# Two-layer gated cross-attention and expert kernel: loads of 100, 116, 119 and 121 rows are issued as a piece of a multiple of sixteen rows and a rest

## The chip, the cores and the metric

One core of a Trainium2 chip runs the whole program. The metric is the device time of one execution in microseconds (us). The core has five instruction streams: TensorE (PE, with its weight loads listed apart as PEld), VectorE (DVE), ScalarE (ACT), GpSimd (POOL) and SyncE (SP). SP computes nothing here: it issues nearly all the transfers, in order, and the transfers run on the core's 16 DMA engines. POOL issues a few transfers too, above all the scatters by row index.

## The reference

The input `x` is 8 batches of 100 tokens of 256 numbers, all float32, with a context of 8 x 361 rows of 256. Four blocks follow one another; `g_xattn` and `g_ffn` give a gate for each, applied through tanh.

```python
def _L0_xattn_ref(query, key, value, mask, Wq, bq, Wk, bk, Wv, bv):
    Q = jnp.einsum('nkm,dm->nkd', query, Wq) + bq
    Kp = jnp.einsum('nkm,dm->nkd', key, Wk) + bk
    V = jnp.einsum('nkm,dm->nkd', value, Wv) + bv
    scores = jnp.einsum('nqd,nkd->nqk', Q, Kp) / jnp.sqrt(jnp.float32(DQ))
    scores = jnp.where(mask, jnp.float32(-1000000000.0), scores)
    w = jax.nn.softmax(scores, axis=2)
    y = jnp.einsum('nqk,nkd->nqd', w, V)
    return y
...
    shared = jax.nn.silu(x @ w_gate.T) * (x @ w_up.T) @ w_down.T
    out = shared + expert_out.sum(axis=0)
```

1. Layer 0 cross-attention over the context with one head, with a mask.
2. Layer 0 feed-forward: a shared gated unit and 16 experts, of which each token takes the one with the highest router logit.
3. Layer 1 cross-attention over the context with 16 heads of 16.
4. Layer 1 feed-forward, itself a block: rotary self-attention with 16 heads, then a normalisation, a shared gated unit of 512 and 8 experts in 2 groups of 4. A token belongs to one group, takes two experts of it, and the sum goes through an RMS normalisation and is added to the token.

## The kernel before, in words

The kernel is one block with a stream for each engine. Order is written out by hand: every dependence is a semaphore, and a transfer adds 16 to its semaphore when it has landed. A token tile has 100 rows (`T = 100`), one for each batch, eight in all, and rows are tokens: `x` and `hN` are 100 rows of 8 x 256. The context is cut into pieces of 121, 121 and 119 rows (`KEYS = 121`). The experts of the last block work on tokens sorted by group, in eight tiles of 116 rows (`ET = 116`, `NX = 8`).

**The start** (SP L403 to L424). SP issues `x`, then the constants, three weights of 256 KB, the two biases, the gates and the bias row `row_bv`, then the mask and the context in three groups of batches, each group two transposed loads and three loads of rows (L412, L415). TensorE's first instruction waits for the weights and the constants together:

```python
pe.wait_ge(s("ld_w0"), 64)
pe.wait_ge(s("ld_const"), 64)
```

The last load that these two count is `row_bv`. DVE's first instruction (L1068) waits for `x` alone, POOL (L616) for the mask, and TensorE's scores for each group of the context.

**Between the layers** (SP L494 to L499, DVE L1206 to L1217). The first layer's experts scatter their rows to `yt_dram`. When the last scatter has landed, SP loads them back as tokens into `hN`, in two halves of four batches. DVE adds a half to `x` (`second_residual`, L1211), takes the statistics (L1050), POOL takes the root (L606) and DVE normalises (L1063). TensorE transposes the rows (L1509) and makes the queries, which go out to `qx_dram` and come back in another layout before the second attention starts.

**Before the sorted experts** (SP L561 to L564). POOL scatters the tokens, each row with 256 numbers, its token number and ten logits, to `es_dram` in sorted order (L734). When all have landed, SP loads them back in four pairs of tiles of 116 rows into `sorted_rows`, a part of `ctxbuf`. Each pair has a semaphore `b_xg`. Meanwhile TensorE makes the second product of the shared unit, 64 recorded products with `wdn`. Then, pair by pair, TensorE transposes (L1990) and ACT copies the result out (L1018); pair g must wait until ACT has emptied the bank of pair g - 2. DVE, after adding the shared result to the tokens (L1421, eight times), waits for all four pairs:

```python
for g in range(NX // 2):
    dve.wait_ge(s(f"b_xg{g}"), 32)
```

and begins the routing: the token numbers (L1424), the maxima and differences of the logits (L1425 to L1431, then `e_gx`), the exponentials on ACT behind its four copies (L1021, which loads an activation table first), and a chain of some 25 small DVE operations up to the weights of the experts (L1464). Only then does DVE multiply the hidden units (L1468). TensorE has made the hidden units of the first three of eight units of work by then and can go no further: the fourth needs a bank that the first L1468 empties.

**The end** (SP L569 to L588). `load_base` (L570) and `load_rest` (L574) bring the shared results and the tokens in sorted order, four loads each of 116 rows, used by DVE at L1475 and L1493. POOL scatters the result (L754).

Of the kernel before, what the change touches and what calls it, by code (L numbers as in the profile page):

```python
# [19 lines left out]
KT = D // 128  # L20
KEYS = 121
NJ = 3
# [36 lines left out]
Y_BANKS = [4, 5, 2, 3, 6, 7, 0, 1]  # L59
HIDDEN = [3 * 4, 3 * 4 + 2, 3 * 4 + 3] + [4 * 4] * 5  # L60


# [100 lines left out]
def build(nc, A, out):  # L163
# [4 lines left out]
    with ctx:  # L168
# [233 lines left out]
        def _(sp):  # L402
            sp.dma_start(x[:], A["x"]).then_inc(s("ld_x"), 16)  # L403
            sp.dma_start(consts[:], A["consts"]).then_inc(s("ld_const"), 16)
# [4 lines left out]
            def load_context(g):  # L409
                a, z = GROUPS[g]  # L410
                for k in range(KT):
                    sp.dma_start(ctxT[:, k, a:z, 0:CTX], A["ctxT"][128 * k:128 * k + 128, a:z]).then_inc(s(f"ld_ctx{g}"), 16)  # L412
                for j in range(NJ):
                    n = min(KEYS, CTX - KEYS * j)
                    sp.dma_start(ctxN[0:n, a:z, j, :], A["ctx"][a:z, KEYS * j:KEYS * j + n, :].rearrange("b p d -> p b d")) \  # L415
                        .then_inc(s(f"ld_ctx{g}"), 16)

            for i, n in enumerate(("g_xattn", "g_ffn")):
                sp.dma_start(gates[:, 2 * i:2 * i + 2], A[n].partition_broadcast(128)).then_inc(s("ld_const"), 16)
            sp.dma_start(brow["bv"][:], A["L0_xattn_bv"].partition_broadcast(128)).then_inc(s("ld_const"), 16)  # L420
            sp.dma_start(mask8[:], A["mask"]).then_inc(s("ld_mask"), 16)
            sp.wait_ge(s("filled"), FILL["pads"])
# [73 lines left out]
            for half in range(2):  # L496
                sp.dma_start(hN[:, NB // 2 * half:NB // 2 * (half + 1), :],
                             yt_dram[HALF * half:HALF * (half + 1), :].rearrange("(b t) d -> t b d", t=T)) \
                    .then_inc(s(f"b_yt{half}"), 16)  # L499
            def load_k(b, part):  # L500
# [61 lines left out]
            for g in range(NX // 2):  # L562
                sp.dma_start(sorted_rows[0:ET, 2 * g:2 * g + 2, :],
                             es_dram[2 * ET * g:2 * ET * (g + 1), :].rearrange("(i p) d -> p i d", p=ET)).then_inc(s(f"b_xg{g}"), 16)  # L564
            sp.wait_ge(s("e_bst"), 16 * (NB + 1))
# [3 lines left out]
            def load_base(g):  # L569
                sp.dma_start(hF[0:ET, 2 * g:2 * g + 2], eb_dram[2 * ET * g:2 * ET * (g + 1), :].rearrange("(i p) d -> p i d", p=ET)) \  # L570
                    .then_inc(s(f"ld_F{g}"), 16)

            def load_rest(g):
                sp.dma_start(xF[0:ET, 2 * g:2 * g + 2], ex_dram[2 * ET * g:2 * ET * (g + 1), :].rearrange("(i p) d -> p i d", p=ET)) \  # L574
                    .then_inc(s("ld_x"), 16)

# [14 lines left out]
        def _(pool):  # L591
# [19 lines left out]

            pool.wait_ge(s("ld_mask"), 16)
            for b in range(NB):
# [423 lines left out]
        def _(dve):  # L1037
# [27 lines left out]

            dve.wait_ge(s("ld_x"), 16)
            for b in range(NB):
# [140 lines left out]
            def second_residual(half):  # L1208
                dve.wait_ge(s(f"b_yt{half}"), 16)
                for b in range(NB // 2 * half, NB // 2 * (half + 1)):  # L1210
                    nc.vector.scalar_tensor_tensor(out=x[:, b, :], in0=hN[:, b, :], scalar=tg[0:T, 2:3], in1=x[:, b, :],  # L1211
                                                   op0=ALU.mult, op1=ALU.add).then_inc(s("b_res"), 1)
# [209 lines left out]
            for g in range(NX // 2):  # L1422
                dve.wait_ge(s(f"b_xg{g}"), 32)
            nc.vector.tensor_copy(tok[0:ET, :], sorted_rows[0:ET, :, D]).then_inc(s("b_tok"), 1)  # L1424
# [45 lines left out]
            for i in range(NX):  # L1470
                dve.wait_ge(s(f"ld_F{i // 2}"), 16)
                for p in range(2):
                    v = 2 * i + p
                    dve.wait_ge(s("e_down"), NB + v + 1)
                    link(nc.vector.scalar_tensor_tensor(out=hF[0:ET, i, :], in0=PB[Y_BANKS[v % 8]][0:ET, 0:D], scalar=we[:, i, 2 * p:2 * p + 1],  # L1475
                                                        in1=hF[0:ET, i, :], op0=ALU.mult, op1=ALU.add))
                    if v == 2 * NX - 1:
                        dve.wait_ge(s("e_down"), NB + v + 2)
                    nc.vector.scalar_tensor_tensor(out=hF[0:ET, i, :], in0=PB[Y_BANKS[(v + (v == 2 * NX - 1)) % 8]][0:ET, D:2 * D], scalar=we[:, i, 2 * p + 1:2 * p + 2],
                                                   in1=hF[0:ET, i, :], op0=ALU.mult, op1=ALU.add).then_inc(s("e_comb"), 1)  # L1480
                    dve.wait_ge(s("e_comb"), v + 1)
                for part, (a, z) in enumerate(FPARTS):
                    if i != z - 1:
                        continue
                    dve.wait_ge(s("f_sq"), z)
                    nc.vector.tensor_scalar(stdF[:, a:z], rsumF[:, a:z], 1.0 / D, RMS_EPS, ALU.mult, ALU.add) \
                        .then_inc(s("n_var"), 1)
                    dve.wait_ge(s("n_std"), roots("f", part))
                    dve.wait_ge(s("ld_x"), 16 * (1 + NX // 2))
                    for k in range(a, z):  # L1490
                        link(nc.vector.scalar_tensor_tensor(out=hF[0:ET, k, :], in0=hF[0:ET, k, :], scalar=rstdF[:, k:k + 1],
                                                            in1=growF[0:ET], op0=ALU.mult, op1=ALU.mult))
                        nc.vector.tensor_tensor(xF[0:ET, k, :], xF[0:ET, k, :], hF[0:ET, k, :], ALU.add).then_inc(s("f_out"), 1)  # L1493
# [3 lines left out]
        def _(pe):  # L1497
# [52 lines left out]
            for i in range(NB + 4):  # L1550
# [9 lines left out]
                if i < NB:  # L1560
                    b = i
                    if b >= 3:
                        pe.wait_ge(s("a_max"), b - 2)
                    for g, (a, z) in enumerate(GROUPS):
                        if a == b:
                            pe.wait_ge(s(f"ld_ctx{g}"), 16 * (KT + NJ))
                    for n in range(KT):
                        last = mm(PB[SB[b % 3]][0:T, 0:CTX], tT[:, n, T * b:T * b + T], ctxT[:, n, b, 0:CTX],
                                  n == 0, n == KT - 1)
                    last.then_inc(s("a_s"), 1)  # L1570
# [126 lines left out]
            pe.wait_ge(s("ld_wc"), 16 * 7)  # L1697
            pe.wait_ge(s("ld_ctx0"), 16 * (KT + NJ + KT))

# [125 lines left out]
            for half in range(3):  # L1825
                for _ in BEFORE[half][n if half == 0 else 0:]:
                    if EARLY[n] == KS[BACK[1][0]][0]:
                        pe.wait_ge(s("ld_ctx1"), 16 * (KT + NJ + KT))
                    early(n)
                    n += 1  # L1830
# [150 lines left out]
            for g in range(NX // 2):  # L1981
                pe.wait_ge(s(f"b_xg{g}"), 32)
                if g < 2:
# [90 lines left out]
```

## Time and profile before

| what | us |
|---|---|
| median of 3 runs | 556.81 (556.79 to 558.48) |
| the profiled execution, its own time | 556.68 |
| its span | 554.9 |
| PE busy in the span | 503.3 (91%) |
| DVE busy | 277.3 (50%) |
| ACT busy | 188.4 (34%) |
| POOL busy | 160.9 (29%) |

The execution's own time is 1.78 us above its span: what lies around the span is not in the trace. Times in the trace count from the span's start. The profiled execution lies 0.13 us below the median of the runs, so what is predicted from its trace stands for the median too. The largest of the three runs lies 1.67 us above the other two.

### The profile page before, as it was taken

What the parts mean: (1) busy time and instruction counts of PE and PEld (TensorE: products, weight loads), DVE (VectorE), ACT (ScalarE), POOL (GpSimd) and SP (SyncE); (2) the same over time, 40 slices, a digit from 0 to 9 for tenths busy, and PEclk for the clock granted to TensorE, in tenths of its full rate; (3) what the DMA queues carried; (4) which work ended last, traced back from release to release, by engine and by line L of the source; (5) the groups of instructions that cost most, each with busy time, mean ns of one, the idle gap of its engine ahead of it and who ended that gap; (6) DMA issues with size and microseconds to landing.
All of it is one profiled execution on the core that took longest, in us unless ns stands there. A gap on an engine that the chain in (4) does not pass through costs nothing.

```text
span 554.9 us, 9313 instructions
## 1 busy us (share of the span) xinstructions
PE 503.3 (91%) x3392; PEld 334.6 (60%) x3392; DVE 277.3 (50%) x664; ACT 188.4 (34%) x443; POOL 160.9 (29%) x179
## 2 busy tenths in 40 slices
PE   1989889899999889999999989899999988999992
PEld 1636565445556558887877767778867564444441
DVE  2436553112222767565576877988743214323452
ACT  1233331121112436555555554646652103110000
POOL 3122005001016306422241562543200666000232
PEclk9799978999999999999999999999999997999997
DMA  8978992269976987887555209300000233002100
GB/s 220 220 200 282 389 335 57 80 215 395 386 258 210 257 187 211 217 203 186 144 138 138 55 2 332 124 2 2 2 1 0 68 129 121 18 17 68 27 11 24
DMA packets 51790, 82.33 MB, mean 148 GB/s; under 512 B 10340, under 2 KB 40428, under 8 KB 51643
## 3 DMA queue, kind: packets, MB, share of 16 engines
q1 hardware_dynamic: 45967, 69.58, 42.2%
q0 software_dynamic: 5776, 12.13, 6.9%
q8 instruction: 29, 0.48, 0.4%
q14 instruction: 18, 0.15, 0.1%
HBM read 66.87 MB, written 15.15 MB: 148 GB/s over the span
## 4 chain that ended last, share of the span: by engine, by line
PE 73%; DVE 12%; issue 4%; DMA 4%; ACT 2%; SPq 1%; POOL 1%; POOLq 0%; DVEq 0%; ACTq 0%
PE pb L1499 68%; DVE hN L1063 2%; DVE nmx L1360 1%; DMA row_bv<-in_L_xattn_bv 1%; DMA qx_dram<-big_r 1%; DVE prob L1363 1%; PE pb L1910 1%; DMA hN<-yt_dram 1%; DVE bn L1050 1%; POOL rstd L606 1%; PE pb L1770 1%; DVE ctxbuf L1290 1%; PE pb L1680 1%; DVE nmx L1268 1%; DVE x L1211 1%
## 5 line engine op out<-in xcount | busy, mean ns | idle before, releaser
L1499 PE MATMUL pb<-split 128*100 128x362 f32 (+2 forms) x320 | 77.5, 326 | 4.0 <-DVE nmx L1268 2.7
L1499 PE MATMUL pb<-ring,big 128*116 (+1 forms) x232 | 76.8, 578 | 1.1 <-ACT big L822 1.1
L1268 DVE TENSOR_REDUCE nmx<-pb 100x1 f32<-100x361 f32 x128 | 62.8, 527 | 21.4 <-PE pb L1499 20.9
L1499 PEld LDWEIGHTS pb<-split 128*100 128x100 f32 (+2 forms) x320 | 55.5, 181 | 13.7 <-DVE nmx L1268 5.3
L1499 PEld LDWEIGHTS pb<-ring,big 128*116 128x116 f32 (+1 forms) x232 | 31.2, 162 | 43.2 <-issue 40.6
L939 ACT ACTIVATE big<-pb 121x400 f32<-121x400 f32 (+1 forms) x96 | 48.3, 505 | 20.5 <-PE pb L1499 17.9
L691 POOL TENSOR_TENSOR shift<-consts,nmx 100x400 fp32r<-100x400 f32 x32 | 28.2, 882 | 75.0 <-DVE nmx L1268 74.9
L1499 PE MATMUL pb<-big,arena 121*32 121x100 f32 (+3 forms) x1072 | 47.4, 261 | 1.7 <-ACT arena L789 1.2
L1499 PEld LDWEIGHTS pb<-big,arena 121*32 121x32 f32 (+3 forms) x1072 | 28.7, 112 | 18.2 <-issue 6.9
L1499 PE MATMUL pb<-hT,wgu 128*128 128x400 f32 (+1 forms) x100 | 35.8, 505 | 0.3 <-DVE hN L1346 0.3
L1499 PE MATMUL pb<-shift 100*121 100x400 f32 (+1 forms) x96 | 35.0, 364 | 0.0
L606 POOL TENSOR_TENSOR rstd<-std,minus_half 100x2 f32<-100x2 f32 (+3 forms) x11 | 11.0, 1000 | 71.9 <-DVE std L1058 46.0
L1499 PE MATMUL pb<-wdn,big 128*100 128x256 f32 x128 | 29.2, 380 | 1.4 <-issue 1.4
L1499 PE MATMUL pb<-ctxbuf 128*100 128x100 f32 x256 | 28.0, 253 | 0.0
L1499 PE MATMUL pb<-big,ring 128*128 128x464 f32 x64 | 27.8, 596 | 0.2 <-DVE big L1468 0.2
L1499 PEld LDWEIGHTS pb<-ctxbuf 128*100 128x100 f32 x256 | 26.1, 168 | 1.4 <-issue 0.8
L1499 PEld LDWEIGHTS pb<-hT,wgu 128*128 128x128 f32 x100 | 19.5, 206 | 12.1 <-issue 3.1
L660 POOL TENSOR_TENSOR ctxbuf<-tT,consts 128x1600 f32<-128x1600 f32 x8 | 24.4, 3045 | 7.4 <-PE pb L1499 7.4
L1499 PEld LDWEIGHTS pb<-wdn,big 128*100 128x100 f32 x128 | 20.8, 167 | 7.4 <-issue 2.0
L638 POOL DMA_INDIRECT yt_dram<-arena,tok x8 | 7.8, 978 | 59.3 <-ACT arena L841 59.3
L1499 PE MATMUL pb<-arena 128*100 128x256 f32 (+1 forms) x40 | 11.9, 433 | 13.6 <-DMA row_bv<-in_L_xattn_bv 12.0
L982 ACT ACTIVATE prob<-prob 100x400 f32<-100x400 f32 x32 | 17.2, 539 | 19.5 <-DVE prob L1363 19.2
(274 smaller groups left out, 844.1 us busy)
## 6 DMA issues: line engine op xcount, KB each, us to landing
ring<-in_L_ffn_gate_up_proj SPq DMA_DIRECT2D x12, 1024.0 KB, 10.1
split<-kx_dram SPq DMA_DIRECT2D x64, 181.0 KB, 3.9
ring<-in_L_ffn_down_proj SPq DMA_DIRECT2D x12, 512.0 KB, 7.9
kx_dram<-split POOLq DMA_DIRECT2D x16, 362.0 KB, 4.0
ctxbuf<-in_L_ffn_gate_up_proj SPq DMA_DIRECT2D x4, 1024.0 KB, 10.3
ring<-in_L_ffn_W_experts SPq DMA_DIRECT2D x4, 1024.0 KB, 13.3
split<-qx_dram SPq DMA_DIRECT2D x64, 50.0 KB, 2.1
ctxbuf<-in_ctxT SPq DMA_DIRECT2D x6, 361.0 KB
```

The lines of the kernel that those rows point to most:

```text
L606: nc.gpsimd.tensor_tensor(to[:, a:z], var[:, a:z], minus_half[0:var.shape[0], a:z], ALU.pow) \
L638: nc.gpsimd.indirect_dma_start(yt_dram, bass.IndirectOffsetOnAxis(tok[:, i:i + 1], 0), yb[:, i % 2, :], None, bounds_check=NT - 1, oob_is_ ...
L660: nc.gpsimd.tensor_tensor(qbd[:, b % 2].rearrange("p k (h t) -> p k h t", h=8), q, m, ALU.mult) \
L691: nc.gpsimd.tensor_tensor(diag[:, t % 2].rearrange("t (h q) -> t h q", h=4), ident[0:T, 0:T].unsqueeze(1).to_broadcast([T, 4, T]), nmx[:, ...
L939: nc.scalar.activation(pTq[0:KEYS_OF[j], t % 2, j, :], PB[ST[j]][0:KEYS_OF[j], 0:4 * T], ACT.Exp) \
L982: nc.scalar.activation(prob4[:, n % 3, :], prob4[:, n % 3, :], ACT.Exp).then_inc(s("d_p"), 1)
L1050: nc.vector.bn_stats(bn6[:, b, :], x[:, b, :]).then_inc(s("stats"), 1)
L1063: nc.vector.tensor_scalar(hN[:, b, :], x[:, b, :], mv[:, b, 0:1], rstd[:, b:b + 1], ALU.subtract, ALU.mult).then_inc(s("n_hN"), 1)
L1211: nc.vector.scalar_tensor_tensor(out=x[:, b, :], in0=hN[:, b, :], scalar=tg[0:T, 2:3], in1=x[:, b, :], op0=ALU.mult, op1=ALU.add).then_inc ...
L1268: nc.vector.tensor_reduce(nmx[:, t % 4, q:q + 1], PB[SB[n % 3]][0:T, 0:CTX], AX.X, ALU.max, negate=True) \
L1290: link(nc.vector.tensor_tensor(w4, w4, sin, ALU.mult))
L1499: return nc.tensor.matmul(o, l, r, start=start, stop=stop)
```

## The change

Every load whose number of rows sixteen does not divide is issued as two: one of the largest multiple of sixteen rows, one of the rest. A helper gives the two ranges of rows. The waits count two transfers where they counted one. Nothing else is changed: no bytes are added, no load changes its place in the order, and the rest follows right behind its piece in SP's stream. Names and lines in the text are those of the kernel before.

```diff
+def by16(rows):
+    return [(0, rows // 16 * 16), (rows // 16 * 16, rows)]
...
-            sp.dma_start(x[:], A["x"]).then_inc(s("ld_x"), 16)
+            for a, z in by16(T):
+                sp.dma_start(x[a:z], A["x"][a:z]).then_inc(s("ld_x"), 16)
...
-                    sp.dma_start(ctxN[0:n, a:z, j, :], A["ctx"][a:z, KEYS * j:KEYS * j + n, :].rearrange("b p d -> p b d")) \
-                        .then_inc(s(f"ld_ctx{g}"), 16)
+                    for p, q in by16(n):
+                        sp.dma_start(ctxN[p:q, a:z, j, :], A["ctx"][a:z, KEYS * j + p:KEYS * j + q, :].rearrange("b p d -> p b d")) \
+                            .then_inc(s(f"ld_ctx{g}"), 16)
...
-            sp.dma_start(mask8[:], A["mask"]).then_inc(s("ld_mask"), 16)
+            for a, z in by16(T):
+                sp.dma_start(mask8[a:z], A["mask"][a:z]).then_inc(s("ld_mask"), 16)
...
-                sp.dma_start(hN[:, NB // 2 * half:NB // 2 * (half + 1), :],
-                             yt_dram[HALF * half:HALF * (half + 1), :].rearrange("(b t) d -> t b d", t=T)) \
-                    .then_inc(s(f"b_yt{half}"), 16)
+                for a, z in by16(T):
+                    sp.dma_start(hN[a:z, NB // 2 * half:NB // 2 * (half + 1), :],
+                                 yt_dram[HALF * half:HALF * (half + 1), :].rearrange("(b t) d -> t b d", t=T)[a:z]) \
+                        .then_inc(s(f"b_yt{half}"), 16)
...
-                sp.dma_start(sorted_rows[0:ET, 2 * g:2 * g + 2, :],
-                             es_dram[2 * ET * g:2 * ET * (g + 1), :].rearrange("(i p) d -> p i d", p=ET)).then_inc(s(f"b_xg{g}"), 16)
+                for a, z in by16(ET):
+                    sp.dma_start(sorted_rows[a:z, 2 * g:2 * g + 2, :],
+                                 es_dram[2 * ET * g:2 * ET * (g + 1), :].rearrange("(i p) d -> p i d", p=ET)[a:z]) \
+                        .then_inc(s(f"b_xg{g}"), 16)
...
-            dve.wait_ge(s("ld_x"), 16)
+            dve.wait_ge(s("ld_x"), 32)
...
-                dve.wait_ge(s(f"b_xg{g}"), 32)
+                dve.wait_ge(s(f"b_xg{g}"), 48)
```

`load_base` and `load_rest` are cut in the same way, into 112 and 4 rows. In all, 25 loads become two each: `x`, the mask, nine of the context, two of `yt_dram`, four each of `es_dram`, `eb_dram` and `ex_dram`.

## Rows read from the trace of the kernel before

**Rows 1.** The page, part 1: busy us (share of the span) and instructions by engine.

```profile
PE 503.3 (91%) x3392; PEld 334.6 (60%) x3392; DVE 277.3 (50%) x664; ACT 188.4 (34%) x443; POOL 160.9 (29%) x179
```

**Rows 2.** The chain that ended last: start us, us, what; to the first scores.

```profile
4.94 6.95 DMA row_bv<-in_L_xattn_bv
12.03 5.47 PE pb L1499 x28
20.83 10.77 PE pb L1499 x24
```

**Rows 3.** The same chain, between the layers.

```profile
175.26 4.66 DMA hN<-yt_dram
```

**Rows 4.** The same chain, before the sorted experts, to its last long piece.

```profile
458.31 3.00 issue
461.88 1.28 ACT L1021
473.17 70.80 PE pb L1499 x176
```

**Rows 5.** Timeline: start, us, instruction, idle before and releaser.

```profile
0.74 0.41 SPq L403 DMA_DIRECT2D x<-in_x  x1
8.16 2.71 DVE L1068 BATCH_NORM_STATS2 bn<-x 100x6 f32<-100x256 f32 x8 [8.16 <-DMA x<-in_x]
21.39 8.17 SPq L415 DMA_DIRECT2D big<-in_ctx  x3
44.06 1.38 PE L1499 MATMUL pb<-ctxbuf,tT 128*100 128x361 f32 x4
512.60 0.48 DVE L1491 SCALAR_TENSOR_TENSOR ctxbuf<-ctxbuf 116x256 f32<-116x256 f32 x1 [1.07 <-POOL ctxbuf L606]
```

**Rows 6.** Windows: stretch, length, busy by engine, granted clock, DMA share, GB/s.

```profile
0.00:12.00 12.00, 0.00 (x0) 0.01 (x1) 3.52 (x17) 0.04 (x1) 2.88 (x13) 1.00 0.81 215
2.50:3.50 1.00, 0.00 (x0) 0.00 (x0) 0.00 (x0) 0.00 (x0) 0.85 (x6) 1.00 0.49 180
8.00:12.00 4.00, 0.00 (x0) 0.01 (x1) 3.52 (x17) 0.04 (x1) 0.09 (x1) 1.00 1.01 300
18.90:25.70 6.80, 6.11 (x16) 3.53 (x15) 2.04 (x1) 1.64 (x4) 0.00 (x0) 0.50 1.03 231
177.00:179.00 2.00, 2.00 (x11) 1.71 (x10) 0.54 (x1) 1.01 (x3) 2.00 (x9) 1.00 0.66 201
```

**Rows 7.** Windows, the same columns, at 206.6 and around the sorted experts' start.

```profile
206.60:210.00 3.40, 3.40 (x14) 3.24 (x15) 2.22 (x5) 1.09 (x3) 2.49 (x4) 0.51 0.40 91
454.80:459.20 4.40, 0.62 (x4) 0.40 (x4) 0.00 (x0) 1.11 (x2) 3.25 (x4) 0.99 0.46 147
459.20:466.00 6.80, 5.76 (x11) 3.15 (x12) 3.40 (x22) 3.40 (x4) 5.28 (x6) 0.50 0.41 120
461.06:473.01 11.95, 11.95 (x26) 5.40 (x24) 6.79 (x35) 4.51 (x6) 6.11 (x7) 0.80 0.34 104
```

**Rows 8.** Timeline between the layers, the columns of group 5.

```profile
185.82 1.20 PE L1509 MATMUL pb<-consts,hN 100*128 100x100 f32 x8 [1.48 <-DVE hN L1063]
203.64 0.70 PE L1499 MATMUL pb<-split 128*100 128x362 f32 x3 [1.16 <-DMA split<-qx_dram]
```

**Rows 9.** Timeline before the sorted experts, the same columns.

```profile
444.89 4.66 SPq L563 DMA_DIRECT2D ctxbuf<-es_dram  x4
453.25 1.09 DVE L1421 TENSOR_TENSOR hN<-pb,arena 100x256 f32<-100x256 f32 x3 [0.36 <-PE pb L1499]
454.14 0.62 PE L1990 MATMUL pb<-consts,ctxbuf 116*128 116x116 f32 x4 [0.23 <-issue]
460.24 1.04 PE L1990 MATMUL pb<-consts,ctxbuf 116*128 116x116 f32 x4 [2.52 <-DMA ctxbuf<-es_dram]
460.31 0.17 DVE L1424 CAST tok<-ctxbuf 116x8 int32<-116x8 f32 x1 [5.97 <-DMA ctxbuf<-es_dram]
```

**Rows 10.** Issues of transfers: name, queue, count, KB each, us to landing.

```profile
ring<-in_L_ffn_W_shared_in SPq DMA_DIRECT2D x1, 1024.0 KB, 5.0
```

More of the change, by code:

```diff
@@ L569, in load_base @@
             def load_base(g):
-                sp.dma_start(hF[0:ET, 2 * g:2 * g + 2], eb_dram[2 * ET * g:2 * ET * (g + 1), :].rearrange("(i p) d -> p i d", p=ET)) \
-                    .then_inc(s(f"ld_F{g}"), 16)
+                for a, z in by16(ET):
+                    sp.dma_start(hF[a:z, 2 * g:2 * g + 2],
+                                 eb_dram[2 * ET * g:2 * ET * (g + 1), :].rearrange("(i p) d -> p i d", p=ET)[a:z]) \
+                        .then_inc(s(f"ld_F{g}"), 16)
             def load_rest(g):
-                sp.dma_start(xF[0:ET, 2 * g:2 * g + 2], ex_dram[2 * ET * g:2 * ET * (g + 1), :].rearrange("(i p) d -> p i d", p=ET)) \
-                    .then_inc(s("ld_x"), 16)
+                for a, z in by16(ET):
+                    sp.dma_start(xF[a:z, 2 * g:2 * g + 2],
+                                 ex_dram[2 * ET * g:2 * ET * (g + 1), :].rearrange("(i p) d -> p i d", p=ET)[a:z]) \
+                        .then_inc(s("ld_x"), 16)
             load_base(0)
@@ L610, in _ @@
             inverse_root("a")
-            pool.wait_ge(s("ld_mask"), 16)
+            pool.wait_ge(s("ld_mask"), 32)
             for b in range(NB):
@@ L1208, in second_residual @@
             def second_residual(half):
-                dve.wait_ge(s(f"b_yt{half}"), 16)
+                dve.wait_ge(s(f"b_yt{half}"), 32)
                 for b in range(NB // 2 * half, NB // 2 * (half + 1)):
@@ L1470, in _ @@
             for i in range(NX):
-                dve.wait_ge(s(f"ld_F{i // 2}"), 16)
+                dve.wait_ge(s(f"ld_F{i // 2}"), 32)
                 for p in range(2):
@@ L1488, in _ @@
                     dve.wait_ge(s("n_std"), roots("f", part))
-                    dve.wait_ge(s("ld_x"), 16 * (1 + NX // 2))
+                    dve.wait_ge(s("ld_x"), 16 * (2 + NX))
                     for k in range(a, z):
@@ L1565, in _ @@
                         if a == b:
-                            pe.wait_ge(s(f"ld_ctx{g}"), 16 * (KT + NJ))
+                            pe.wait_ge(s(f"ld_ctx{g}"), 16 * (KT + 2 * NJ))
                     for n in range(KT):
@@ L1697, in _ @@
             pe.wait_ge(s("ld_wc"), 16 * 7)
-            pe.wait_ge(s("ld_ctx0"), 16 * (KT + NJ + KT))
+            pe.wait_ge(s("ld_ctx0"), 16 * (KT + 2 * NJ + KT))
             def keys_values(piece, bank):
@@ L1827, in _ @@
                     if EARLY[n] == KS[BACK[1][0]][0]:
-                        pe.wait_ge(s("ld_ctx1"), 16 * (KT + NJ + KT))
+                        pe.wait_ge(s("ld_ctx1"), 16 * (KT + 2 * NJ + KT))
                     early(n)
@@ L1981, in _ @@
             for g in range(NX // 2):
-                pe.wait_ge(s(f"b_xg{g}"), 32)
+                pe.wait_ge(s(f"b_xg{g}"), 48)
                 if g < 2:
```

## The prediction

> **What bounds the kernel now.** I read the page first: TensorE is busy in 91% of the span [rows 1]. So a load matters only where TensorE stands still for it, or where what it lets start leads to TensorE. The chain of waits names where a load that the change cuts, or one queued behind it, is on the path: at the start [rows 2], between the layers [rows 3] and before the sorted experts [rows 4]. The windows then tell how many DMA engines work there, since the DMA share is a mean over 16 of them. From 2.5 to 3.5 us, when little but `x` can be under way, the share is 0.49; during the load of `hN` it is 0.66, at 201 GB/s [rows 6]. Ten busy engines of 16 would be 0.63, so I read a load of 100 rows as ten engines with ten rows each: the engines that can have equal shares. That the number of engines must divide the number of rows is my inference from this. By it 116 rows get four engines, and indeed the four loads of `es_dram`, issued from 444.89, have the last of them landed only at 460.24 [rows 9].
>
> Against this, TensorE's first product at 12.03 waits for `row_bv` [rows 2], with all 16 engines busy in front of it (share 1.01 at 300 GB/s from 8 to 12 us, [rows 6]). There the question is not idle engines but whose work stands ahead on the ten that carry `x`.
>
> In the numbers below 0.3% is about what a measurement of this kernel can tell from no change: 1.7 us.
>
> **Before the sorted experts.** The four loads move 4 x 242 KB, 0.99 MB. Issued at 444.89, they landed by 460.24, 15.4 us later [rows 9]. Cut, and by the inference above, each is 112 rows over 16 engines and 4 rows over four. The nearest row is a single load of 1024 KB with rows of 4 KB, which lands in 5.0 us [rows 10]. Eight issues at 0.41 us each [rows 5] put the last one at 444.89 + 7 x 0.41 = 447.8, so I expect the last landing between 450.4 (2.6 us behind the last issue, the part of a landing that is not bytes, worked out for `hN` below) and 452.8 (5.0 us behind it). Both ends lie ahead of the next bound: TensorE makes its products with `wdn` until about 453.5, DVE adds the last shared result at 453.25 + 1.09 = 454.34, and TensorE's transposes of pair 1 end at 454.14 + 0.62 = 454.76 [rows 9]. The load then stands before nobody.
>
> What follows, step by step. Transposes of pair 2 at 454.8 to 455.4, ACT's copy of it to 456.1; pair 3's at 455.4 to 456.0, ACT's copy to 456.8 (0.62 us for four transposes; 0.6 for a copy, as the last transposes end at 460.24 + 1.04 = 461.28 and the table load behind the copy begins at 461.88, [rows 4, 9]). ACT's table load for the exponentials starts when the fourth copy is done: 461.88 now [rows 4], 456.8 then, 5.1 us earlier. DVE is released even more, 460.31 to 454.4 [rows 9], 5.9 us, but it needs those exponentials, so ACT sets 5.1. The DVE chain behind it is unchanged, and what now lets TensorE go on at 473.17 [rows 4] does so at 468.1. The 70.8 us behind it hold no load in the chain [rows 4] and move as a whole. **Term: 5.1 us.** Bounds: 5.9 if ACT's copies go faster than I laid them; 4.2 if the last load lands at 456, 4.2 us earlier than now.
>
> What is late next: TensorE's first three units. They took 11.95 us at a granted clock of 0.80 [rows 7], that is 9.6 at full clock. Begun at 456.1, they end at 465.7, and TensorE then stands for 2.4 us where it now stands for nearly nothing. That is no loss in itself, but see the rivals.
>
> **The start.** What must land for TensorE: `x` 800 KB, constants 246.5, three weights of 256, biases and gates 4, `row_bv` 128: 1946.5 KB or 1.99 MB. Moved in 12 us: 12 x 215 = 2.58 MB [rows 6]. So 0.59 MB that nobody waits for went first, on the engines without a share of `x`. With `x` on all 16 engines that comes behind; at 300 GB/s [rows 6] it is 1.9 us. The four rows of rest hold 8 KB each and lie on four engines, which carry 7 rows and not 6.25: 0.75 x 8.2 KB at 300/16 = 19 GB/s, 0.3 us back. That leaves 1.6 us. The issue of the rest (0.41 us, [rows 5]) is covered, as the queues are full when `row_bv` is issued. DVE's side keeps pace: `x` is seen at 8.16 [rows 5] and should be seen some 2 us earlier.
>
> But the clock was at its lower level, 1.2 GHz, from 18.9 to 25.7 [rows 6], within the products from 20.83 to 31.60 [rows 2]. If that stretch stays where it is, products begun 1.6 us earlier lie in it for 1.6 us longer at half speed, and 0.8 us are given back. I take the lower value, since the row shows the stretch. **Term: 0.8 us.** Bounds: 2.0 (no give-back, and the rest costs nothing) and -0.4 (no gain, and the issue delays all behind it).
>
> **Between the layers.** The first half of `hN` (400 KB) landed 4.66 us after its issue [rows 3]. At 201 GB/s [rows 6] its bytes take 0.41 MB / 201 = 2.0 us; the other 2.6 are there in either form. An engine's share falls from 40 packets of 1 KB (ten rows of four) to 24, or 28 on the four that carry the rest too: 30% of 2.0 is 0.6 us. The second issue of 0.41 us runs beside the first piece's work. DVE starts 0.6 us earlier, and both places where TensorE waits for this chain have more than that to give: 1.48 us for DVE's normalised rows and 1.16 us for the queries' way back [rows 8]. **Term: 0.6 us.** Bounds: 0.8 and -0.4 (the issue alone).
>
> **What costs nothing.** The mask and nine context loads add ten issues, 4.1 us of SP's time. The last context load is issued by 29.56 and first used at 44.06 [rows 5]: 14 us of cover, and without it the cost would be the 4.1. `eb_dram` and `ex_dram` add eight issues; DVE's first use of the latter at 512.60 was released by POOL's root and not by the load [rows 5]. If the cover fails, an issue of 0.41 us is the price.
>
> **Sum.** 5.1 + 0.8 + 0.6 = 6.5 us. The profiled execution took 556.68, 0.13 below the median: 556.7 - 6.5 = **550.2 us**.
>
> **A rule against it.** The rows speak of engines left without work, which two pieces fill. The Trainium skill ("DMA: Bandwidth & Descriptors", section "Rules for kernel authors") advises against this form: two transfers to disjoint halves of the partitions serialise, since both spray over all 16 engines, and one transfer should be used. By that rule every gain would be nil. It speaks of loads of 128 rows, though, and the same page ("Why a DMA increments its semaphore by 16 and not by 1") has the count of engines divide the rows, 10 for 100, which the share of 0.66 agrees with; for 116 rows its rule gives 4, which no single row here isolates.
>
> **The rivals.**
>
> *The clock falls in the new gap* (0.20). Before the sorted experts TensorE was busy 0.62 of 4.4 us, and then had the lower clock for 6.8 us [rows 7]; this cost nothing, as the DVE chain was as long. In the changed kernel the gap of 2.4 us lies right before 70.8 us in which TensorE sets the end. A low stretch costs half its length: the shortest in these rows is 3.4 us at 206.6, the long one 6.8 [rows 7], so 1.7 to 3.4, in the middle 2.6: 552.8 us. Against it: one gap of 2.4 us behind 9.6 us of work, where the row shows two gaps with little between them.
>
> *The start and `hN` bring nothing* (0.10): the packets of 16 engines slow one another, and only the issues are left. 5.1 - 0.4 - 0.4 = 4.3 us: 552.4. For it: at 3.5 us and later all engines are busy whatever carries `x`.
>
> *More than the sum* (0.06): the low stretches at 18.9 or 206.6 shrink by one of 3.4 us because work has moved: 1.7 us more, and the start's 0.8 back: 547.7.
>
> *Slower: the pieces do not run side by side* (0.04). If the time of a load is set by its source or by POOL's scatters that share the engines (in `es_dram` every row has just been written by one), a load in two pieces takes as long as in one and the issues come on top. Place: four more issues ahead of the last `es_dram` landing, 1.6 us on a path with no slack, and 0.4 each at the start and at `hN`: 556.7 + 2.4 = 559.1. It decides when the last `es_dram` landing comes after 460.2; any landing before 458 makes the sum positive. Against it: 0.99 MB in 15.4 us is 64 GB/s, where other stretches move 200 to 300 [rows 6].
>
> The forecast itself has 0.60.
>
> **How the numbers follow.** From the forecast down: 2.0 and 0.8 for the small terms and one vanished low stretch give 556.7 - 5.1 - 2.8 - 1.7 = 547.1. Up: the first two rivals lie at 552.8 and 552.4, and 3.4 us of low clock with the forecast's terms at 553.6. Range 547.1 to 553.6; outside remain the slower case, half of the case of more than the sum, and mixtures of the two middle rivals. Faster by over 0.3%: all cases but the last and its neighbours, 0.94. Within 0.3%: 0.03. Slower: 0.03. The last two are the slower rival's 0.04, three parts of it over the bound, and 0.02 of the mixtures around the bound.
>
> **What would show each step.** In the profile after: the last L1990 and L1424 released by DVE's or TensorE's own work and no longer by `es_dram`, L1424 near 454 and ACT's table load near 457; TensorE idle for some 2 us before its fourth unit. The DMA share from 2.5 to 3.5 us near 0.8 and more, DVE's first instruction near 6, TensorE's near 10.5. The wait before DVE's first L1211 shorter by 0.6. The forecast is wrong if the transposes of pairs 2 and 3 still wait for a load, or if TensorE's long piece before the end runs at the lower clock.

## The result, and the profile after

The changed kernel took **549.56 us** (median of 3, 548.61 to 550.51) against 556.81: ratio 0.9858, 95% interval 0.9836 to 0.9879. The ratios of this text are estimates over all runs of both kernels, so they differ a little from the quotient of two medians (0.9870 here). Of the kernel with all but `x` cut, further down, two of seven runs were slow, 849.54 and 1013.16 us, and stand outside its ratio. The forecast was 550.2. The profiled execution took 549.56 with a span of 547.8; against the span of 554.9 before, 7.1 us went. The page, part 1 (compare [rows 1]):

```profile
span 547.8 us, 9338 instructions
PE 501.7 (92%) x3392; PEld 335.1 (61%) x3392; DVE 277.2 (51%) x664; ACT 187.5 (34%) x443; POOL 160.8 (29%) x179
```

Busy times hardly moved; what shrank is waiting, and time at the lower clock. The chain that ended last (start us, us, what), at the three places of [rows 2, 3, 4]. The lines of TensorE, DVE and ACT lie 15 further down than before (L1499 is now L1514), those of SP some ten:

```profile
5.36 5.76 DMA row_bv<-in_L_xattn_bv
...
11.26 7.13 PE pb L1514 x28
...
22.19 10.33 PE pb L1514 x24
...
176.52 3.37 DMA hN<-yt_dram
...
192.14 7.49 DMA qx_dram<-big_r
...
440.46 14.05 PE pb L1514 x64
...
456.69 9.35 PE pb L1514 x24
466.04 0.15 issue
466.19 70.80 PE pb L1514 x176
```

Before the sorted experts no load is in the chain any more; TensorE goes from the products with `wdn` to its long last piece with a wait of 0.34 us for ACT's copy and one of 0.15 us. The long piece begins with the fourth unit of work, at 466.19 against 473.17. The timeline of that place (start, us, instruction, idle before and releaser), beside [rows 5, 9]:

```profile
445.87 3.04 SPq L573 DMA_DIRECT2D ctxbuf<-es_dram  x8
...
454.35 0.96 PE L2005 MATMUL pb<-consts,ctxbuf 116*128 116x116 f32 x8
...
454.89 0.16 DVE L1439 CAST tok<-ctxbuf 116x8 int32<-116x8 f32 x1
...
455.65 1.04 PE L2005 MATMUL pb<-consts,ctxbuf 116*128 116x116 f32 x8 [0.34 <-ACT big L1033]
...
457.30 1.28 ACT L1036 ACT_TABLE_LOAD   x1
```

Eight issues took 3.04 us where four took 4.66. The transposes of pairs 2 and 3 wait only for ACT's copy, and DVE begins the routing right behind its own last addition.

The windows (length, busy by engine, granted clock, DMA share, GB/s), beside [rows 6, 7]:

```profile
0.00:12.00 12.00, 0.74 (x2) 0.68 (x3) 3.52 (x17) 0.80 (x1) 3.85 (x13) 1.00 0.86 217
2.50:3.50 1.00, 0.00 (x0) 0.00 (x0) 0.00 (x0) 0.00 (x0) 0.84 (x6) 1.00 0.97 303
177.00:179.00 2.00, 2.00 (x10) 1.58 (x9) 0.93 (x2) 0.85 (x2) 2.00 (x8) 1.00 0.80 234
446.00:449.00 3.00, 3.00 (x16) 2.32 (x15) 0.42 (x1) 0.00 (x0) 2.39 (x3) 1.00 0.80 234
456.52:466.04 9.52, 9.52 (x26) 4.39 (x24) 6.29 (x31) 4.71 (x7) 7.39 (x8) 1.00 0.45 132
```

In the kernel before, the stretch from 446 to 449 us reads:

```profile
446.00:449.00 3.00, 3.00 (x15) 2.34 (x14) 0.42 (x1) 0.00 (x0) 2.29 (x3) 1.00 0.35 112
```

From 2.5 to 3.5 us the share is 0.97 where it was 0.49. While `es_dram` is loaded it is 0.80 at 234 GB/s where it was 0.35 at 112. And the first three units, 24 products together, ran at a granted clock of 1.00 in 9.52 us, where they took 11.95 us at 0.80.

Where the 7.1 us came from, by the two traces:

| stretch | before | after | change |
|---|---|---|---|
| start to first scores | 33.17 | 34.09 | +0.9 |
| to the first of the 64 products with `wdn` | 439.46 | 440.46 | +1.0 in all |
| from there to the fourth unit | 33.71 | 25.73 | -8.0 |
| from there to the end | 81.7 | 81.6 | -0.1 |

So the forecast for the whole, 6.5 us, was 0.6 us off. Its terms were further off: it had 5.1 + 0.8 + 0.6. The experiments had to say what each cut is worth, and why one is worth more and two nothing.

### The profile page after: what moved, and what is told of

The parts are those of the page before. It is cut to its first block, busy times and chain, and to the rows that moved or that the text cites. A ratio compares the mean times of both kernels' runs of the same rounds, so it can differ in the third digit from the quotient of the medians.

```text
span 547.8 us, 9338 instructions
## 1 busy us (share of the span) xinstructions
PE 501.7 (92%) x3392; PEld 335.1 (61%) x3392; DVE 277.2 (51%) x664; ACT 187.5 (34%) x443; POOL 160.8 (29%) x179
## 4 chain that ended last, share of the span: by engine, by line
PE 76%; DVE 11%; DMA 4%; issue 3%; ACT 2%; SPq 1%; POOL 1%; POOLq 0%; DVEq 0%; ACTq 0%
PE pb L1514 70%; DVE hN L1078 2%; DMA qx_dram<-big_r 1%; DVE nmx L1375 1%; DMA row_bv<-in_L_xattn_bv 1%; DVE prob L1378 1%; PE pb L1925 1%; DVE bn L1065 1%; POOL rstd L621 1%; PE pb L1785 1%; DVE ctxbuf L1305 1%; PE pb L1524 1%; PE pb L1695 1%; DVE nmx L1283 1%; DMA hN<-yt_dram 1%
## 5 line engine op out<-in xcount | busy, mean ns | idle before, releaser
L1514 PE MATMUL pb<-split 128*100 128x362 f32 (+2 forms) x320 | 77.4, 326 | 5.2 <-DVE nmx L1283 2.7
L1514 PE MATMUL pb<-ring,big 128*116 (+1 forms) x232 | 76.8, 578 | 1.1 <-ACT big L837 1.1
L1514 PEld LDWEIGHTS pb<-split 128*100 128x100 f32 (+2 forms) x320 | 55.3, 180 | 15.0 <-DVE nmx L1283 5.3
L1514 PEld LDWEIGHTS pb<-ring,big 128*116 128x116 f32 (+1 forms) x232 | 31.2, 162 | 43.2 <-issue 40.6
L954 ACT ACTIVATE big<-pb 121x400 f32<-121x400 f32 (+1 forms) x96 | 48.1, 504 | 21.6 <-PE pb L1514 18.9
L1514 PE MATMUL pb<-big,arena 121*32 121x100 f32 (+3 forms) x1072 | 47.4, 261 | 1.7 <-ACT arena L804 1.2
L1514 PEld LDWEIGHTS pb<-big,arena 121*32 121x32 f32 (+3 forms) x1072 | 28.7, 112 | 18.2 <-issue 6.9
L1514 PE MATMUL pb<-hT,wgu 128*128 128x400 f32 (+1 forms) x100 | 35.5, 501 | 0.3 <-DVE hN L1361 0.3
L1514 PE MATMUL pb<-shift 100*121 100x400 f32 (+1 forms) x96 | 34.8, 362 | 0.0
L1514 PE MATMUL pb<-wdn,big 128*100 128x256 f32 x128 | 29.2, 380 | 1.4 <-DVE big L1392 1.4
L1514 PE MATMUL pb<-ctxbuf 128*100 128x100 f32 x256 | 28.0, 253 | 0.0
L1514 PEld LDWEIGHTS pb<-ctxbuf 128*100 128x100 f32 x256 | 26.1, 168 | 1.4 <-issue 0.8
L1514 PEld LDWEIGHTS pb<-hT,wgu 128*128 128x128 f32 x100 | 19.3, 204 | 11.9 <-issue 2.8
L1514 PE MATMUL pb<-big,ring 128*128 128x464 f32 x64 | 25.3, 554 | 0.2 <-issue 0.2
L1514 PEld LDWEIGHTS pb<-wdn,big 128*100 128x100 f32 x128 | 20.8, 167 | 7.4 <-DVE big L1392 2.0
L1514 PE MATMUL pb<-arena 128*100 128x256 f32 (+1 forms) x40 | 12.1, 436 | 12.8 <-DMA row_bv<-in_L_xattn_bv 11.3
```

The costliest lines, as they stand in the source:

```text
L954: nc.scalar.activation(pTq[0:KEYS_OF[j], t % 2, j, :], PB[ST[j]][0:KEYS_OF[j], 0:4 * T], ACT.Exp) \
L1514: return nc.tensor.matmul(o, l, r, start=start, stop=stop)
```

## The experiments

Each kernel takes the changed kernel's helper with a switch for each group of loads, so the waits follow. Ratios are to the kernel before on the same chip, with 95% intervals; "median" is of that kernel's own runs. The medians of the kernel before lay between 557.9 and 559.0 us there, so compare ratios and not times. The traces of these kernels count lines 26 above the kernel before (L1499 is L1525, L1990 is L2016, L1424 is L1450, L1021 is L1047), except for the full change repeated, which has the lines of after.

### One part alone: x, hN, es_dram, eb_dram with ex_dram

```diff
 # x alone; the three others in the same way
-            sp.dma_start(x[:], A["x"]).then_inc(s("ld_x"), 16)
+            for a, z in by16(T, "x"):
+                sp.dma_start(x[a:z], A["x"][a:z]).then_inc(s("ld_x"), 16)
```

> Only the load of x is cut (96 and 4 rows). Theory A (the lower clock at the start eats the earlier landing): TensorE's first product begins 0.6 to 1.0 us earlier than in the kernel before (12.03, with the full change 11.26), but the first scores (33.17 before, 34.09 with the full change) come 0 to 1 us later when the products before them run wholly at the lower clock; total 0 to +1 us, 556.8 to 557.8. Rival B (the loads behind x, cut too, are what delayed the scores): the scores come at 32.4 and the total is 556.0.

> Only the two loads of hN are cut (96 and 4 rows). Both theories: hN is there 0.8 us earlier (4.66 us after its issue before). Theory A (the way of the queries back through qx_dram stands in the DMA queues behind kx_dram's loads, which do not move): the landing of the queries stays within 0.3 us of where it was against the last scatter, and the total is 556.8 +- 0.5. Rival B (my term of the prediction): the second attention starts 0.6 to 0.8 us earlier and the total is 556.1.

> Only the four loads of es_dram are cut (112 and 4 rows), eb_dram's and ex_dram's stay whole. The landing of all four comes before DVE's last shared result. Theory A (the small DVE operations of the routing stood still for 2.4 us because eb_dram's whole loads crowd four DMA engines): 5.5 us are gained, 551.3, and gaps of about 2.4 us in sum between the DVE operations remain or move. Rival B (the gaps came from somewhere else and vanish as everything before them is earlier): 8 us gained, 548.8.

> Only the loads of eb_dram and ex_dram are cut; es_dram's stay whole, so TensorE and DVE still wait for them until 460. Theory A (eb_dram's whole loads stop the DVE operations): DVE's routing loses its gaps and is up to 2.4 us shorter, but TensorE's first three units (11.95 us, begun at 461) then set the end of the stage, so the total is 556.8 less 0 to 0.3, and L1468 starts some 2 us earlier while TensorE does not. Rival B: the gaps stay, total 556.8.

| cut alone | median | ratio |
|---|---|---|
| `x` (10 runs) | 556.98 | 0.9981 (0.9957 to 1.0004) |
| `hN` (10) | 557.74 | 0.9989 (0.9958 to 1.0020) |
| `es_dram` (9) | 550.76 | 0.9876 (0.9844 to 0.9909) |
| `eb_dram`, `ex_dram` (10) | 558.59 | 1.0005 (0.9978 to 1.0032) |

`es_dram` alone gives the whole change (0.9858), within the intervals. The fourth unit begins 25.73 us after the first product with `wdn`, as in after. Its timeline:

```profile
441.09 14.05 PE L1525 MATMUL pb<-wdn,big 128*100 128x256 f32 x64 [1.35 <-DVE big L1403]
...
446.50 3.06 SPq L584 DMA_DIRECT2D ctxbuf<-es_dram  x8
...
457.16 9.52 PE L1525 MATMUL pb<-big,ring 128*128 128x464 f32 x24
457.93 1.28 ACT L1047 ACT_TABLE_LOAD   x1
...
466.82 3.38 PE L1525 MATMUL pb<-big,ring 128*128 128x464 f32 x8 [0.15 <-DVE big L1494]
```

At this place the kernel with only `eb_dram` and `ex_dram` cut is the kernel before. Its chain:

```profile
449.71 14.32 DMA ctxbuf<-es_dram
464.07 1.04 PE pb L2016 x4
465.11 27.30 PE pb L1525 x65
```

and its timeline and one window:

```profile
473.22 0.23 DVE L1488 TENSOR_TENSOR ctxbuf<-ctxbuf 116x64 f32<-116x64 f32 x1
...
473.97 1.19 DVE L1494 TENSOR_TENSOR big<-sil,pb 128x464 f32<-128x464 f32 x2
```

```profile
464.90:476.42 11.52, 11.52 (x27) 5.55 (x26) 7.73 (x37) 4.51 (x6) 3.95 (x4) 0.83 0.36 107
```

In the kernel before, for comparison:

```profile
469.55 0.22 DVE L1460 TENSOR_TENSOR ctxbuf<-ctxbuf 116x64 f32<-116x64 f32 x1 [1.21 <-DVE ctxbuf L1459]
...
472.48 1.96 DVE L1468 TENSOR_TENSOR big<-sil,pb 128x464 f32<-128x464 f32 x3
473.17 7.27 PE L1499 MATMUL pb<-big,ring 128*128 128x464 f32 x18 [0.16 <-DVE big L1468]
```

This decides how the 8.0 us is to be read. In the profiled execution of before, DVE's small operations stood apart by 2.57 us in five gaps (0.40, 0.24, 1.21, 0.25 and 0.47), and TensorE's fourth unit seemed released by DVE. Here, with `es_dram` whole as well, the gaps are not there and DVE is ready at 473.97. Still the 24 products end only at 476.42, since TensorE, at a granted clock of 0.83, needs 11.52 us for them. Counted from the first product with `wdn` to the end of these 24, it takes 33.67 us here, 33.55 in before and 33.4 in the `hN` kernel. So two things bounded the stage at once: late landings, and a TensorE that after waiting for them ran its next products at half clock for some microseconds. My expectation that `eb_dram`'s whole loads held DVE back fell: with them whole, the profiles of the `es_dram` and the `hN` kernel have no such gaps either. What made the gaps is not known. In before they cost next to nothing, as TensorE's own products ended at 473.01 anyway.

Read by TensorE's path, the 8.0 us are 5.5 us of an earlier start of the 24 products within the stage (21.60 us behind the first product with `wdn` before, 16.06 after) and 2.43 us of clock. In after, DVE's first product with the hidden units ends at 466.13 and TensorE's 24 products end at 466.04. From here on either of them sets the time.

`x` alone: first product at 10.88, as against 12.00, 12.31 and 12.44 in the three others of this batch. The scores come at 33.96, as against 33.42, 34.02 and 35.92. The gain at the first product is there; what follows below is why it doesn't show in the time.

`hN` alone: DVE begins with the first half 3.94 us after the issue of its first piece, where it was 4.69. (The chain has 3.53 here, but counts from the issue of the rest, 0.39 us later.) But from the issue of the last scatter to the queries' landing in `qx_dram` it took 26.44 us, against 25.46 in before, 25.77 and 25.79 in the `es_dram` and `eb_dram` kernels and 27.03 in the `x` kernel, all four with `hN` whole. The queries' store itself took 7.63 us, against 6.20 in before and 6.62 to 6.90 in the three others.

### The number of engines: es_dram in 58 and 58, and in 64 and 52 rows

```diff
 # in effect; the kernels have a switch here
-    first = rows // 16 * 16          # 112 + 4
+    first = 58                       # and, in another kernel, 64
```

> Only the four loads of es_dram are in two pieces, but of 58 and 58 rows. Theory A (a load's engines are the largest number up to 16 that divides its rows, here 2, and always the same first ones): the loads get slower than whole (4 engines): 0.99 MB over two engines at the 19 GB/s an engine had in the whole form is 26 us, so the last lands some 28 us behind the first issue instead of 15, and the total is 556.8 + 12 = 569. Rival B (it is the being in two pieces that runs side by side, whatever the rows): it lands as with 112 and 4, total 550.

> Only es_dram's loads in two pieces, of 64 and 52 rows. Theory A (largest number up to 16 that divides the rows: 16 and 13 engines): 0.99 MB spread over 13 to 16 engines lands well before DVE's last shared result, as with 112 and 4 rows; total as e3_es, 551. Rival B (only a piece of four rows or a first piece of nearly all rows does it): lands later than 456, over 553.

58 and 58: **569.67** (two runs), ratio 1.0215 (1.0151 to 1.0279), for the same number of transfers and the same bytes. The timeline:

```profile
446.49 18.10 SPq L584 DMA_DIRECT2D ctxbuf<-es_dram  x8
...
455.70 0.62 PE L2016 MATMUL pb<-consts,ctxbuf 116*128 116x116 f32 x4 [0.66 <-DMA ctxbuf<-es_dram]
...
461.56 1.04 PE L2016 MATMUL pb<-consts,ctxbuf 116*128 116x116 f32 x4 [5.24 <-DMA ctxbuf<-es_dram]
...
468.05 1.03 PE L2016 MATMUL pb<-consts,ctxbuf 116*128 116x116 f32 x4 [5.45 <-DMA ctxbuf<-es_dram]
...
474.77 1.03 PE L2016 MATMUL pb<-consts,ctxbuf 116*128 116x116 f32 x4 [5.69 <-DMA ctxbuf<-es_dram]
```

A pair of tiles lands every 6.4 us or so, twice the 3.1 us between the last pairs of the whole loads (457.10 and 460.24 in before). The last pair lands 28.3 us after the first issue; the expectation of two engines had some 28. SP's eight issues are stretched to 18.10 us; that a full queue holds the next issue back is my reading. 64 and 52: 550.96 (two runs), 0.9875 (0.9826 to 0.9924), with the stage at 25.74 us. So what counts is not that there are two pieces, nor that they are large and small, but a count that 16 or 13 engines can share. Two engines for 58, four for 116, ten for 100 are all the largest divisor of the rows that is not above 16. The trace does not list the engines of a load; the rule is inferred from the shares and the landings, and fits all four forms of `es_dram` that ran (whole, 58 and 58, 64 and 52, 112 and 4). The rule of the Trainium skill that the prediction weighed ("DMA: Bandwidth & Descriptors", section "Rules for kernel authors"), one transfer and not two for disjoint halves of the partitions, doesn't carry over from 128 rows to 116: by it 64 and 52 would have gained nothing, and they gained 1.25%. That loads of 128 rows gain nothing was not run.

### Where the gain of hN goes: the keys' load behind the queries' stores

The stores of the queries to `qx_dram` stand on SP's queue behind two groups of four loads of keys from `kx_dram`. The first kernel has `hN` cut and puts the second of these groups behind the stores; the other kernel has the full change as well.

```diff
-            for part in range(2):
-                load_k(0, part)
+            load_k(0, 0)
...
+            load_k(0, 1)
```

> hN's loads cut as in e2_hN, and besides the loads of the second half of the heads' keys of batch 0 (four of eight loads of 181 KB from kx_dram) are issued behind the four stores of the queries to qx_dram, not in front. Theory A (the stores stood behind them in the DMA queues, which took hN's gain): the queries' stores land 1 us or more earlier, 24.9 us or less behind the last scatter's issue (25.5 before, 26.4 in e2_hN), and the second attention starts by so much earlier, total 1 us under e2_hN's. Rival B (stores of 400-byte rows take 6 to 7.5 us anyway): no earlier, total as e2_hN.

> The full change and the later key loads of e9_k_late. Theory A: 0.5 to 1 us faster than the full change alone, 548.8. Rival B: the same as the full change.

With `hN` alone cut: 559.37, 1.0023 (0.9988 to 1.0058). With all cut: 550.41, 0.9872 (0.9827 to 0.9916). From the last scatter's issue to the queries' landing the first of the two took 24.06 us, 2.4 less than the `hN` kernel. Its chain, and then that of the `hN` kernel:

```profile
178.09 3.56 DMA hN<-yt_dram
...
193.85 5.42 DMA qx_dram<-big_r
...
202.47 4.81 DMA split<-qx_dram
```

```profile
176.30 3.53 DMA hN<-yt_dram
...
192.32 7.63 DMA qx_dram<-big_r
...
203.15 1.99 DMA split<-qx_dram
```

The store is 2.2 us shorter and the load that follows 2.8 us longer. Where `hN`'s gain goes is seen at TensorE's two waits, beside [rows 8] (the kernel of the result):

```profile
185.80 1.21 PE L1524 MATMUL pb<-consts,hN 100*128 100x100 f32 x8 [0.65 <-DVE hN L1078]
...
204.92 0.72 PE L1514 MATMUL pb<-split 128*100 128x362 f32 x3 [2.46 <-DMA split<-qx_dram]
```

The first wait shrank from 1.48 to 0.65 us and the second grew from 1.16 to 2.46. In the eight profiles with `hN` cut the first is 0.44 to 0.92 us and the second 2.42 to 3.20; in the six with `hN` whole they are 1.02 to 2.19 and 1.16 to 2.31. So between the layers, what is gained on one transfer is paid on a later one. The queue is busy there: the DMA share is 1.22 from 192 to 198 us in before. That this is the reason fits both experiments but is not shown by itself.

From the last scatter's issue to the steady part of the second attention it took 54.23 us in before, 54.34 in after and 54.45 in the full change with the later key loads. In three kernels, all with `hN` cut, it took 56.4 to 56.5; their stretch at the lower clock from 203 to 210 us was 6.83 and not 3.41 us long. Whether that comes with the cut is open, as five others with `hN` cut do not have it.

### The full change once more, and without x

> The full change once more, for more runs. Theory: what the cuts give is the sum of es_dram's (7.7 us from the start of the 64 products with wdn to TensorE's fourth unit: 33.7 before, 25.7 after), and x's (about 1 us at the landing of row_bv), the rest nothing; 549.6 to 551. The times spread by the phase of the lower clock at the start: the step from the first product to the first scores is 21.1 to 23.5 us by execution, in this kernel as in the one before. Rival: the full change is faster than es_dram's cut alone by more than 1.5 us, so the small cuts matter.

> The full change with x whole. Theory A: row_bv lands 0.9 us later than with x cut (12.2, not 11.3), and that is all that x is worth; on the average of many executions 0.5 to 1.5 us slower than the full change (e11_full 0.9865 of the kernel before, so 0.988 to 0.989). Rival B: the earlier start is always lost again to the lower clock, 0.9865.

The full change: 550.03, 0.9865 (0.9817 to 0.9912). All but `x`: 551.84 (median of five), 0.9887 (0.9848 to 0.9926). The first product came at 11.46 with `x` cut and 13.07 without. The difference of the ratios is 0.002, smaller than either interval, so a worth of `x` of about 1 us is neither shown nor excluded. The mask and the nine context loads were not run alone.

### The start in another order

If `x` lands earlier, TensorE's first product still waits for `row_bv`, which it doesn't need. So here the constants are issued behind the weights and biases, and the wait for them stands where TensorE transposes, with all 25 loads cut:

```diff
-            sp.dma_start(consts[:], A["consts"]).then_inc(s("ld_const"), 16)
...
+            sp.dma_start(consts[:], A["consts"]).then_inc(s("ld_const"), 16)
...
             pe.wait_ge(s("ld_w0"), 64)
-            pe.wait_ge(s("ld_const"), 64)
...
+            pe.wait_ge(s("ld_const"), 64)
```

> The full change, and the constants are issued behind the weights and biases, and TensorE's first product waits for the weights and biases only; it waits for the constants and row_bv before its transposes. Theory A (the landing is bound by bytes): 376 KB fewer lie ahead, at 280 GB/s 1.3 us, so the first product begins near 10.0 instead of 11.3; the transposes then wait for DVE's normalised rows (17.3 in the full change) and the first scores come 1 us earlier, 549.0. Rival B (latency or the lower clock sets it): first product over 10.8, total as the full change.

> The kernel of the previous start experiment once more, unchanged. There the first scores came 1.7 us earlier than in the full change, the last scatter of the first layer 4.7 us earlier, and the time was 3.7 us less. In that profile TensorE's stretch at the lower clock from 76 us on was 3.4 us long, and 10.2 us in every profile of the full change. Theory A (the order of the loads gives what is seen at the scores, the rest is a matter of where the low stretches fall): the stretch at 76 us is 10.2 us long again or its length changes between executions, and the ratio to the kernel before is near 0.983 (549.5 - 1.7 = 547.8 against 557). Theory B (an earlier start shortens that stretch each time): the stretch is 3.4 us long again, and the ratio is 0.979 again.

First time: **546.37** (545.19 to 548.73), 0.9790 (0.9759 to 0.9822). Second, on another chip: 548.95 (548.09 to 550.84), 0.9848 (0.9809 to 0.9888). The first product waits for `bqk`, the last of what it needs (timeline, second execution):

```profile
9.23 3.78 PE L1525 MATMUL pb<-arena 128*128 128x256 f32 x8 [9.23 <-DMA bqk<-in_bqk]
12.80 3.41 PE L1525 MATMUL pb<-bqk,arena 128*128 128x1 f32 x16
...
16.31 3.18 PE L1535 MATMUL pb<-consts,hN 100*128 100x100 f32 x16
```

Scores began at 32.62 and 32.09, against 34.09 and 34.28 in the full change. Above that, the first of the two had its last scatter issued at 168.97 and the second at 171.66 (full change: 173.67 and 173.85). The windows tell why: first the full change of the result, then the first of the two kernels.

```profile
77.48:87.72 10.24, 10.24 (x34) 7.34 (x35) 5.92 (x24) 3.06 (x4) 0.67 (x1) 0.51 0.00 0
```

```profile
76.42:79.83 3.41, 3.41 (x10) 2.10 (x11) 2.34 (x9) 2.30 (x3) 0.00 (x0) 0.51 0.00 0
79.83:86.66 6.83, 6.83 (x34) 4.32 (x33) 4.48 (x20) 1.01 (x2) 2.26 (x2) 1.00 0.06 15
202.71:209.54 6.83, 6.83 (x25) 6.03 (x25) 4.85 (x11) 2.02 (x4) 4.00 (x5) 0.51 0.65 189
424.58:427.99 3.41, 3.41 (x7) 1.74 (x6) 0.58 (x6) 0.00 (x0) 0.00 (x0) 0.51 0.00 0
```

A stretch at the lower level that was 10.24 or 13.7 us long in all other profiles was 3.41 there; 6.83 us less at half speed saves 3.4. Later the same execution had 3.4 us more of it at 203 us and a stretch of 3.41 us at 424 us that after did not have, together the same 3.4 us back. With the same code the second execution had 10.24 us at 75 again, and the other stretches as in after. Before the sorted experts it lost 0.7 us: DVE's chain had one gap of 0.33 us, and TensorE went on 0.32 us behind the end of DVE's first product, where it is some 0.05 in after:

```profile
464.85 6.49 PE L1525 MATMUL pb<-big,ring 128*128 128x464 f32 x16 [0.82 <-DVE big L1494]
```

So the order of the start gives 1.5 to 2.2 us at the scores, and the rest is where the low stretches fell; I would count on the second result. The profiled one of the first six runs was also their slowest, so the five others may have kept more of the gain at 76 us; they have no trace. Both intervals lie well below the kernel before. Below the full change (0.9865, 0.9817 to 0.9912) the two lie by 0.2% and 0.8%, and the intervals overlap, so that it beats the full change is seen at the scores and likely, but not settled, in the time. It is the fastest version that was run.

## Why the prediction was right, point by point

**How many engines a load gets.** Right as far as the runs can tell: ten for 100 rows, four for 116 was the inference, and the loads in 58 rows landed as two engines would have them (28.3 us, 28 expected). The rival of pieces that don't run side by side is refuted by eight issues in 3.04 us at a share of 0.80.

**Before the sorted experts, 5.1 us: 8.0.** Right in its first half. Transposes ran right behind TensorE's products, the first routing operation came at 454.89 (forecast 454.4) and the table load at 457.30 (456.8). As the stage began 1.0 us later, the table load is 5.6 us earlier within it, against 5.1. The step that failed is "the DVE chain behind it is unchanged": from the table load to the fourth unit it took 11.29 us before and 8.89 after, 2.4 less. I had read five gaps in it as part of the chain, 2.57 us in all. The kernel with `eb_dram` cut shows what stood behind them: TensorE's 24 products, partly at the lower clock, take as long as the chain with its gaps. The sentence "this cost nothing, as the DVE chain was as long" had it the wrong way round. Both had to go for the 8.0 us, and both went. Gaps as in before (2.57 us) are in no other profile; single ones are in two (0.47 us with the later key loads, 0.33 in the second start kernel). That the low stretch cost 2.43 us is shown. Without it a gap costs too, as the second start kernel has it. The 8.0 us need a chain without gaps, which the rows from one execution could not show.

**TensorE idle for 2.4 us before the fourth unit, and the clock falling there (0.20).** Wrong. The gap was 0.15 us, because the DVE chain was 2.4 us shorter; and the granted clock was 1.00 from 456.52 to 466.04 and then to 541.5. The rival had the sign of the clock's part reversed: the cut took a low stretch away. All six profiled kernels with `es_dram` whole or in 58 rows have a stretch at half clock that begins while TensorE waits for these loads, at 459 to 465 us, five of them 6.8 us long and the one of 58 rows 20.5; the eight with `es_dram` in 112 and 4 or 64 and 52 have none there. That is in kind the case of more than the sum (0.06), a low stretch that vanishes, which I had placed at 18.9 or 206.6 with 3.4 us; it came at 459.2 with 6.8. It is worth 2.43 us of TensorE's time (11.95 - 9.52).

**The start, 0.8 us: nothing seen.** `row_bv` released the first product 0.77 us earlier in the profile (11.26 for 12.03). Over the profiles it stands at 10.88, 11.26, 11.46 and 11.47 with `x` cut, and between 11.89 and 13.07 in the eight without: about 1 us, not 1.6. DVE saw `x` at 7.19 for 8.16, 1 us earlier and not 2. The step that failed is that all 0.59 MB which nobody waits for would come behind. TensorE waits for 1.99 MB. Up to its first product 2.58 MB had moved before, at 215 GB/s, and 2.41 MB in after, at 214 GB/s: only 0.17 MB fewer, which at this rate is the 0.8 us seen. The share in that time rose (0.81 to 0.85), the rate did not. Why 0.42 MB still go first is open.

From the first product to the scores, before, the `hN` and the `es_dram` kernel took 21.1 to 21.7 us, all eleven others 22.8 to 23.5. The 16 small products with `bqk` tell them apart: 1.84 to 2.27 us in the three, 3.41 in the eleven. (The eleven profiles have no low stretch on record this early; the products' own times show it.) So in the pair of profiles of the result the start lost 0.9 us, as the give-back was 1.7 and not 0.8. Whether it must come with an earlier first product is open: all six with `x` cut show it, but so do five of eight without. The ratio of `x` alone, 0.9981, includes nothing and up to 2.4 us.

**hN, 0.6 us: nothing seen.** DVE was released 0.90 us earlier after the issue (3.79 for 4.69 us), so the load was priced about rightly. The step that failed is that it goes on to TensorE because "both places where TensorE waits for this chain have more than that to give". I took the wait for the queries' way back as slack that the chain would fill. It grew instead, from 1.16 to 2.46 us, and the landing of the queries was no earlier (25.96 us from the scatter in after, 25.46 before). The ratio of `hN` alone, 0.9989 (0.9958 to 1.0020), would still allow the 0.6 us; the 54.34 for 54.23 us at the place does not show them.

**What costs nothing.** Right. `eb_dram` and `ex_dram` cut alone: 1.0005. Last context load issued by 24.99, earlier than the 29.56 before, though there are more issues: the queue takes them faster.

**The number.** 550.2 against 549.56 came from 6.5 against 7.1 us, but as +2.9 at one term, -1.7 at the start, -0.7 between the layers and +0.1 behind. That these nearly cancelled was luck. A forecast that is right in its total is no proof of its terms; what each is worth came from the single-part kernels and the places in their profiles.

## What to carry to other kernels

Look at the number of partitions of every load that something waits for. Where sixteen does not divide it, the load ran, as far as these runs tell, on as many engines as its largest divisor up to 16 (116: four; 58: two; 100: ten), and a cut into a multiple of sixteen and a rest can give back most of it for an issue of 0.41 us; 64 and 52 rows did as well as 112 and 4. But only a load that nothing else hides pays: of 25 cut loads, four made the gain here.

Before costing a chain of small operations from one execution, look whether it has gaps that end with nothing but the engine's own last operation as releaser; if so, take a second execution before you count them. And where TensorE waits in pieces, add the lower clock that follows the wait to the wait's price.

## What the runs showed of the hardware

- A slow load also holds back the issuing engine: four issues took 4.66 us for 116 rows, eight took 18.10 us in pieces of 58, and 3.04 us in pieces of 112 and 4.
- A wait can cost twice: a stage with 5 us of waiting ran its next 24 products at a granted clock of 0.80 or 0.83 in 11.95 and 11.52 us, and without the wait in 9.52.
- The low stretches differ between executions, in the two of the same code and in kernels that are the same up to that point: 3.41, 10.24 or 13.7 us at 74 to 80 us, 3.41 or 6.83 us at 203 to 210, one of 3.41 or none at 425 to 432. 6.83 us at half speed cost 3.4, and runs of one kernel spread by 3 to 7 us (548.09 to 550.84, 556.28 to 563.66). A cut worth 1 us is hard to see in this kernel's time; it must be seen at the place itself.
